# Attention and sparse feed-forward on one core: three banks for shifted scores, streamed row maxima, projections spread over the units

## What is computed

```python
q = (x @ wq).reshape(bsz, toks, NH, HD)      # NH 32, HD 16
k = (x @ wk).reshape(bsz, toks, NKV, HD)     # NKV 8
v = (x @ wv).reshape(bsz, toks, NKV, HD)
scores = jnp.einsum('bqgrd,bkgd->bgrqk', qg, k) / jnp.sqrt(...)
attn = jax.nn.softmax(scores, axis=-1)
out = jnp.einsum('bgrqk,bkgd->bqgrd', attn, v)
x = _layernorm(x + out.reshape(bsz, toks, NH * HD) @ wo)
idx = jnp.argmax(blk, axis=-1) + jnp.arange(0, INTER, SPARSITY)
x = _layernorm(x + einsum(relu(einsum(w1[idx], x)), w2t[idx]))
```

## Time and profile before

| | us |
|---|---|
| three timed runs | 1003.74, 1004.98, 1006.87 (median 1004.98) |
| the profiled execution | 998.58 |
| its span, first to last instruction | 996.8 |
| TensorE busy | 908.2 (91%) |
| VectorE busy | 562.4 (56%) |
| ScalarE busy | 442.9 (44%) |
| GpSimd busy | 193.1 (19%) |
| mean granted TensorE clock | 0.944 of 2.4 GHz |

### The profile page before, as it was taken

One profiled execution on the slowest core, in us unless ns is written; L12 is line 12 of the kernel. 1 busy time (PEld: TensorE's weight loads), 2 busy tenths in 40 slices (PEclk: granted clock), 3 DMA queues, 4 the chain that ended last, 5 costly groups with the idle time before them and its releaser, 6 DMA issues. The chain is left out here.

```text
span 996.8 us, 12134 instructions
## 1 busy us (share of the span) xinstructions
PE 908.2 (91%) x4472; PEld 533.0 (53%) x4472; DVE 562.4 (56%) x743; ACT 442.9 (44%) x821; POOL 193.1 (19%) x183
## 2 busy tenths in 40 slices
PE   5868999999899998999989975999999999999995
PEld 3745543333334333343333434777777777777774
DVE  4636567888656885468866533545563365326413
ACT  3302466777654775456765542322222222222231
POOL 6302003730210002100021002333321222122221
PEclk8889999999989998599988978999999999999998
DMA  8466535643342243323433124214030002001101
GB/s 249 160 205 240 169 110 159 175 123 91 91 117 69 76 134 80 97 85 79 135 82 109 34 97 102 82 44 155 14 116 11 1 3 103 2 1 43 42 1 42
DMA packets 50858, 92.99 MB, mean 93 GB/s; under 512 B 5648, under 2 KB 13840, under 8 KB 50288
## 3 DMA queue, kind: packets, MB, share of 16 engines
q1 hardware_dynamic: 49312, 87.05, 29.3%
q0 software_dynamic: 1488, 5.16, 1.9%
HBM read 56.80 MB, written 34.87 MB: 92 GB/s over the span
## 5 line engine op out<-in xcount | busy, mean ns | idle before, releaser
L509 DVE TENSOR_REDUCE neg_max<-ps_max 128x2 f32<-128x1024 f32 x256 | 302.9, 1217 | 90.1 <-PE ps_max L670 89.7
L486 ACT ACTIVATE probs<-ps_st 128x512 f32<-128x512 f32 x496 | 270.2, 595 | 142.6 <-PE ps_st L707 139.7
L707 PE MATMUL ps_st<-q,k 50*128 50x512 f32 x496 | 181.9, 511 | 28.5 <-ACT probs L486 27.6
L707 PEld LDWEIGHTS ps_st<-q,k 50*128 50x128 f32 x496 | 71.9, 192 | 203.1 <-ACT probs L486 156.8
L670 PE MATMUL ps_max<-k,q 48*128 48x512 f32 x512 | 152.8, 452 | 14.0 <-DVE neg_max L509 9.2
L721 PE MATMUL ps_pv<-probs,v 128*32 128x512 f32 x1024 | 147.3, 649 | 5.9 <-ACT probs L486 2.3
L978 POOL TENSOR_TENSOR g_l<-picked,g_h 128x512 fp32r<-128x512 f32 x56 | 73.1, 1306 | 286.9 <-ACT g_h L1017 286.9
L1003 ACT ACTIVATE mask_t<-ps_t 128x512 bf16<-128x512 bf16 x56 | 33.4, 597 | 163.6 <-PE ps_t L1199 163.6
L1211 PE MATMUL ps_h<-xt_h,w_h 128*128 128x512 f32 x224 | 93.8, 419 | 8.0 <-ACT relu L1010 8.0
L1073 DVE TENSOR_REDUCE top<-ps_prep 128x14 f32<-128x448 f32 x62 | 38.6, 623 | 99.0 <-PE ps_prep L1188 98.8
L670 PEld LDWEIGHTS ps_max<-k,q 48*128 48x128 f32 x512 | 75.6, 199 | 28.9 <-DVE neg_max L509 13.5
(11 more groups left out here) (159 smaller groups left out, 1141.2 us busy)
## 6 DMA issues: line engine op xcount, KB each, us to landing
q_stacks<-parts SPq DMA_DIRECT2D x48, 256.0 KB
q<-q_stacks SPq DMA_DIRECT2D x64, 192.0 KB, 3.6
sums<-stage SPq DMA_DIRECT2D x32, 256.0 KB, 3.4
k<-k_stacks SPq DMA_DIRECT2D x64, 96.0 KB, 3.1
x_raw<-xT SPq DMA_DIRECT2D x16, 256.0 KB, 8.5
yf<-after_attention SPq DMA_DIRECT2D x4, 1024.0 KB, 5.3
w_raw<-w POOLq DMA_DIRECT2D x16, 224.0 KB, 3.1
w_raw<-w SPq DMA_DIRECT2D x14, 256.0 KB, 2.9
```

The lines of the kernel that those rows point to most:

```text
L486: nc.scalar.activation(probs[kt % 2][:, r], score_bank(n, r), ACT.Exp, scale=float(HD) ** -0.5).then_inc(exp_done, 1)
L509: nc.vector.tensor_reduce(neg_max[n % 2][:, i // 2, :, i % 2], ps_max[i % 2][:], AX.X, ALU.max, negate=True).then_inc(max_red, 1)
L707: nc.tensor.matmul(score_bank(n, r), k_[n % QR][64 * a:64 * a + ROWS, kt * P:(kt + 1) * P], q[n % QR][64 * a:64 * a + ROWS, j, :], start=T ...
```

## The change

`_attend` is written anew in most of its orders; what is computed stays. PSUM in the loop is now `ps_pair` (two banks), `ps_one`, `ps_st` with three banks, `ps_pv`, `ps_x`. Tile i of the shifted scores may start when the exponential of tile i - 3 is done. The row-maximum tiles are one stream over all units: tiles 3m and 3m + 1 go to `ps_pair` and are reduced together, tile 3m + 2 to `ps_one`, alone; one such matmul stands behind each shifted one, 33 tiles ahead of the step's own. The tasks are ordered k, q, v, and only items 0 and 1 are projected ahead of the loop. The other 12 tasks and the 12 output tiles are groups, one per unit (`GROUPS`), each cut in pieces of four matmuls at the end of steps 2, 3 and the next unit's step 0. Output tiles stand in units 14 to 17, 19 to 22 and 28 to 31. The low parts of x for items 1 to 3 and the high parts for items 2 and 3 are made on GpSimd. Scaling and splitting w1 take another order on GpSimd: item 0's scaling, all of w1, item 1's, item 2's. `load_unit` waits for the last shifted score of the buffer's old unit instead of its last weighing. Part of SBUF is laid over other memory.

```diff
-        ps_max = [ps(f"ps_max{j}", [P, 2, S]) for j in range(2)]
-        ps_st = [ps(f"ps_st{j}", [P, S]) for j in range(2)]
-        ps_pv = ps("ps_pv", [P, S])
-        ps_x = ps("ps_x", [P, S])
-        bank = [(*ps_st, ps_pv)[i % 3] if i < FRONT else ps_x for i in range(LAST)]
+        ps_pair, ps_one = ps("ps_pair", [P, 2, S]), ps("ps_one", [P, S])
+        ps_st = [ps(f"ps_st{j}", [P, S]) for j in range(3)]
...
-        NEXT_X = {(0, 2): 1, (0, TASKS - 1): 2, (2, 3): 3}
-
-        LATE_AT = ((0, -1), (0, 2), (1, 0), (1, 2), (2, 0), (2, 2))
-
-        WO_AT = ((5, 0), (5, 2), (6, 0), (6, 2))
-        HIGH_AT = ((3, 2), (3, 3), (4, 0), (4, 1))
+
+        TURN_V = {6: 2, 13: 3}
+        GROUPS = {}
+        for o in range(TASKS):
+            GROUPS[o] = ("task", 2, o)
+            GROUPS[7 + o] = ("task", 3, o)
+        for t in range(TT):
+            GROUPS[14 + t] = ("wo", 0, t)
+            GROUPS[19 + t] = ("wo", 1, t)
+            GROUPS[28 + t] = ("wo", 2, t)
+        SUMS_FROM = (0, 12, 20)
+        HIGH_AT = {(11, r): (0, r) for r in range(REP)} | {(18, 1): (1, 0), (18, 2): (1, 1), (18, 3): (1, 2),
+                                                          (19, 0): (1, 3)} | {(27, r): (2, r) for r in range(REP)}
...
+            for o in range(VTASK):
+                store_part(0, o)
+            load_unit(0)
             for k in range(KT):
                 load_x(2, k)
-            for b in range(NB - 1):
-                for s in range(TASKS):
-                    store_projection(b, s)
-                    if b == NB - 2 and s == SHIFT_TASK:
-                        send_shift(0)
-                    if b == 1 and s in (1, 3):
-                        load_unit(1 + (1, 3).index(s))
-                if b == 0:
-                    load_unit(0)
-                if b == 1:
-                    load_v(0)
-                    load_v(1)
-                    for k in range(KT):
-                        load_x(3, k)
+            load_unit(1)
+            store_v(0)
+            load_unit(2)
+            load_v(0)
+            load_v(1)
+            for o in range(VTASK):
+                store_part(1, o)
+            send_shift(0)
+            store_v(1)
...
+            def row_max(tile):
+
+                dve.wait_ge(max_mm, tile + (2 if tile % 3 == 0 else 1))
+                old = (tile + 1) // TILES - 3
+                if old >= 0:
+                    dve.wait_ge(max_split, old + 1)
+                at = tile % RING
+                if tile % 3 == 0:
+                    nc.vector.tensor_reduce(neg_max[:, at:at + 2], ps_pair[:], AX.X, ALU.max,
+                                            negate=True).then_inc(max_red, 1)
+                else:
+                    nc.vector.tensor_reduce(neg_max[:, at:at + 1], ps_one[:], AX.X, ALU.max,
+                                            negate=True).then_inc(max_red, 1)
+
+            def row_maxima(begin, end):
+
+                for tile in range(begin, end):
+                    if tile % 3 == 1:
+                        row_max(tile - 1)
+                    elif tile % 3 == 2:
+                        row_max(tile)
...
-            def scores(n, i, a):
-
-                if n >= NU:
+            def scores(tile):
+
+                if tile >= NT:
                     return
-                if a == 0:
-                    if i == 0:
-                        pe.wait_ge(unit_in[n % QR], LOADS * DMA * (n // QR + 1))
-                    if 8 * n + i >= 2:
-                        pe.wait_ge(max_red, 8 * n + i - 1)
-                t, j = i // 2, i % 2
-                mm = nc.tensor.matmul(ps_max[i % 2][:, a], q[n % QR][64 * a:64 * a + STACK, j, t * P:(t + 1) * P],
-                                      k_[n % QR][64 * a:64 * a + STACK, :], start=True, stop=True)
-                if a == 1:
-                    mm.then_inc(max_mm, 1)
+                n, i = divmod(tile, TILES)
+                t, j, a = i // 4, i // 2 % 2, i % 2
+                if i == 0:
+                    pe.wait_ge(unit_in[n % QR], LOADS * DMA * (n // QR + 1))
+                if tile >= 3:
+                    pe.wait_ge(max_red, 2 * (tile // 3) - (tile % 3 < 2))
+                dst = ps_one[:] if tile % 3 == 2 else ps_pair[:, tile % 3]
+                nc.tensor.matmul(dst, q[n % QR][64 * a:64 * a + STACK, j, t * P:(t + 1) * P],
+                                 k_[n % QR][64 * a:64 * a + STACK, :], start=True, stop=True).then_inc(max_mm, 1)
...
-                if i < 2:
-                    pe.wait_ge(evacuated, FRONT - 2 + i)
-                elif n < NU - 2 or (n, kt) == (NU - 2, 0):
-                    pe.wait_ge(exp_done, i - 1)
-                    if r == 2 and n == NU - 2:
-                        pe.wait_ge(max_red, 8 * NU)
+                if i < 3:
+                    task_taken(pe, EARLY - 4 + i)
                 else:
-                    pe.wait_ge(exp_done, i - 3)
+                    pe.wait_ge(exp_done, i - 2)
...
+                    step = n * TT + kt
+                    ahead = 4 * step + 33
                     scores_t(n, kt, 0)
-                    if n == 0 and kt == 0:
-                        scores(2, 0, 0)
-                    scores(n + 2, 2 * kt, 1)
+                    scores(ahead)
                     scores_t(n, kt, 1)
-                    if kt or n:
-                        weigh(*divmod(n * TT + kt - 1, TT))
-                    if not b and (g, kt - 1) == LATE_AT[0]:
-                        turn_v(NB - 1)
-                    if not b and (g, kt) in LATE_AT:
-                        pe.wait_ge(shift_ready, n + 1 + (kt > 1))
-                        project(NB - 1, LATE_AT.index((g, kt)))
-                    if b and (g, kt) in WO_AT and n < NU - 2:
-                        project_out(b - 1, WO_AT.index((g, kt)), n + 1 + (kt > 1))
+                    scores(ahead + 1)
                     scores_t(n, kt, 2)
-                    scores(n + 2, 2 * kt + 1, 0)
+                    scores(ahead + 2)
+                    if step:
+                        weigh(*divmod(step - 1, TT))
                     scores_t(n, kt, 3)
-                    scores(n + 2, 2 * kt + 1, 1)
-                    scores(*divmod(8 * (n + 2) + 2 * kt + 2, 8), 0)
-                    if n == NU - 2 and (g, kt) in WO_AT:
-                        project_out(b - 1, WO_AT.index((g, kt)), n + 1 + (kt > 1))
+                    scores(ahead + 3)
+                    if kt == 0:
+                        group(n - 1, 8, 12)
+                    if kt == 1 and n + 1 < NU:
+                        if n == 0:
+                            pe.wait_ge(v_ready, 2)
+                        else:
+                            pe.wait_ge(shift_ready, n + 1)
+                            turned_free(pe, n - 1)
+                        turn_max(n + 1)
+                    if kt == 2:
+                        group(n, 0, 4 if n + 1 < NU else 6)
+                    if kt == 2 and n in TURN_V:
+                        pe.wait_ge(shift_ready, n + 2)
+                        turn_v(TURN_V[n])
+                    if kt == 3:
+                        group(n, 4 if n + 1 < NU else 6, 8 if n + 1 < NU else 12)
...
+            def group(n, begin, end):
+
+                kind, b, i = GROUPS.get(n, ("none", 0, 0))
+                if kind != "none" and begin == 0 and n + 1 < NU:
+                    pe.wait_ge(shift_ready, n + 2)
+                if kind != "none" and begin == 0 and n + 1 == NU:
+                    turned_free(pe, n - 1)
+                if kind == "task":
+                    project(b, i, begin, end)
+                if kind == "wo":
+                    project_out(b, i, begin, end)
...
+            add_tile(NB - 2, TT - 1)
+            variance(NB - 2)
+            norm(NB - 2)
```

597 lines of the change are left out of this document (328 added, 269 removed).

## The result

The changed kernel takes **1066.5 us** (median of four runs, 1051.8 to 1073.8) against 1004.5 for the kernel before (1003.7 to 1006.9): 1.053 times the time before, interval 1.042 to 1.064. The forecast was 983.7 us, faster, in a range of 952 to 1012. The sign was wrong, and the time lies 54 us above the range. The ratio is of fast runs alone: two of the four, the profiled one among them, are slower than the others at a lower mean clock (0.900 and 0.904 against 0.913 and 0.924). The profiled execution took 1073.8 us, span 1072.0. Against the span of before, 996.8, that is +75.2, the upper end of what the change costs, and it divides into stages.

The account below looks back on a forecast made before the run. Two score banks were taken to bound a plain unit (3.10 us chain per step), VectorE second. Start -29, loop +1.7 and end +6 gave 977.3 us, and 6.4 from profiled run to median made 983.7, range 952 to 1012.

Parts of the forecast that it names:

- Part 4: Half-clock stalls in the loop: 31.4 us are such events; with `att` cast later, no such wait is left.
- hand-followed chain: Twelve row-maximum tiles followed over three steps in the loop, weighings included: 9.33 us together, 3.11 per step.
- Part 1: Loop, three score banks and three row-maximum tiles: step 3.11 us (was 3.13), plain unit 13.05 (12.52 before).
- four rounds: Loop's rounds of a pair (A, B) and single C: 1.77 us without weighing; with it 2.03, 2.36, 3.17 (between A, B).
- Part 2: Loop's 24 groups of 12 matmuls in three pieces: 2.8 us per projection group, 3.3 per output tile.
- Part 3: Start, six projections leaving the front: unit 0 lands at 43 us, first exponential at 75 (68 to 90), -29.
- Part 5: End, between loop and feed-forward: the last output tile's work and the store of x1 follow the loop, +6 us.
- (c): Rival: the half clock stays by a new wait, +20 us, 1004 us, no change; chance 0.12.
- (b): Rival, loop's hand-over: a pair's second tile starts a slot late, 0.24 us per round, 1022 us in all; chance 0.13.
- the rule that the prediction set beside this rival: TensorE: only weight loads are pulled ahead of matmuls in flight; by this rule (b) is the case.
- (a): Rival, loop: VectorE at its own pace, weighings hidden behind full banks; plain unit 11 us, 922 us in all; chance 0.12.
- (d): Rival, start: the front gains only half, first exponential at 90 us, 998.7 us in all, still faster; chance 0.10.

Follow-up runs that it names:

- e1: The changed kernel with the next unit's shift sent ahead of the reciprocals on SyncE's queue, as in the kernel before; 1036.9 us, 1.031 times before.
- w1: The changed kernel with the weighing never between the two tiles of a pair, the shift left behind the reciprocals; 1021.2 us, 1.012 times before.
- e2: e1 with the weighing of every third step one tile forward, so that it never splits a pair; 996.2 us, 0.987 times before.
- e4: e1 with all twelve matmuls of a group in one piece at the end of step 2; 1041.3 us, 1.039 times before.
- e5: e2 with VectorE's part of a group earlier: output tile's addition ahead of step 1's maxima, projection's part between their halves; 1030.5 us, 1.025 times before.
- h1: g1 with ScalarE's casts of the second batch item's `att` one step later each; 981.7 us, 0.976 times before.
- b1: The kernel before with only the swap that puts the reciprocals' broadcast ahead of the shift on SyncE's queue; 1038.2 us, 1.028 times before.
- e6: e5 with item 3's loads of x behind unit 3's shift, and GpSimd's loads behind its casts for item 2; 1017.1 us, 1.001 times before.
- g3: g1 with row maxima over 256 of each tile's 512 columns, so the output differs; 961.6 us in one run.
- g1: e2 with e6's two moves of loads and without e5's moves on VectorE; 989.8 us, 0.983 times before.
- h2: h1 with VectorE's normalisation of two batch items cut into four tiles, one per step; 975.2 us, 0.968 times before.

## Why the prediction was wrong

Loop lengths of the profiled executions, the time at half clock in them, and how many waits they hold:

| | span | loop | at half clock | waits of TensorE of 0.7 to 1.3 us | over 1.3 us |
|---|---|---|---|---|---|
| before | 996.8 | 485.7 | 64.0 | 2 | 4 |
| after | 1072.0 | 572.9 | 153.9 | 39 | 5 |
| e1 | 1038.7 | 537.2 | 96.0 | 43 | 3 |
| w1 | 1023.3 | 523.4 | 109.9 | 14 | 5 |
| e2 | 992.1 | 490.6 | 52.8 | 18 | 3 |
| e4 | 1038.8 | 540.6 | 76.1 | 33 | 4 |
| e5 | 1027.6 | 528.4 | 136.9 | 14 | 8 |
| h1 | 980.2 | 483.2 | 52.9 | 15 | 2 |
| b1 | 1036.0 | 520.4 | 133.1 | 2 | 4 |

- **Part 4 is the step that failed.** It said that "no such wait is left in my reading" and took 31.4 us of stalls and half clock out of the loop. Instead 28.2 us of waits for the shift came in, and 153.9 us at half clock, at 0.40 another 62. Without these two the loop is 572.9 - 28.2 - 62 = 483 us (491 at a price of 0.35), and the forecast, which had neither, was 487.7. So the rest of the sum of the loop holds to about 5 us, if only in total (the plain unit was put 0.4 us too short), and the miss there is this part: 31.4 assumed gone, 90 found. It failed in two ways.
- *The queue.* The order on SyncE's queue was read for where the shift stands, not for what stands in front of it. For the reciprocals the prediction asked only when `att` is cast. The kernel before has the two calls in the other order, and e1, e2 against w1, and b1 show that the swap alone is worth 22 to 30 us in either kernel. The Trainium skill (DMA: Bandwidth & Descriptors, Queues, rings and completion order) says that each DMA engine takes one queue's descriptors in order and that a transfer's signal lands after every earlier write of that engine. By this rule a shift behind a megabyte lands with the megabyte, and the traces above agree, 12 to 13 us in the changed kernel and 11.3 in b1.
- *The clock.* The earlier trace rows showed one low stretch behind a wait of 3.20 us, and I took long waits for the only cause. The hand-followed chain itself said that TensorE would wait about once in three steps for a pair. I gave that its length in us and nothing more. In e1, with only two waits over 3 us left in the loop, 96 us of it are at half clock, and in e2, which takes out 25 of the waits of 0.7 to 1.3 us and none of the long ones, 52.8. All four runs of each bear it out: by their mean clocks the half clock in the whole span is 142 to 164 us in e1 and 88 to 146 in e2. The Trainium skill (TensorE: Matmul & The Clock Gate, A second HAM failure mode: psum-queue depth-cycling) describes short idle times between groups of matmuls, while banks are cycled, as enough to bring the clock down; e1 against e2 agrees. It is not their number alone: e5 has 14 such waits and 136.9 us at half clock, e4 has 33 and 76.1, and the kernel before has 77 waits of 0.15 to 0.4 us in its loop and keeps the clock beside them.
- **Part 1, the plain unit.** Forecast 13.05, wrong if over 13.7; measured 13.46 (580.30 to 593.76) in unit 27, the only plain one at full clock. Units 24 to 26, which the prediction named, took 18.5, 21.4 and 15.9 us at mean clocks of 0.58, 0.75 and 0.80, and the second holds the wait of 7.41 us; by the prediction's own sign they are wrong. In e1 the same units take 16.9, 13.6 and 13.6, the last two at full clock. The four rounds as VectorE shows them in unit 27 and 28:

```profile
584.43 1.23 DVE L602 TENSOR_REDUCE neg_max<-ps_pair 128x2 f32<-128x1024 f32 x1 [1.63 <-PE ps_pair L765]
...
586.52 1.23 DVE L602 TENSOR_REDUCE neg_max<-ps_pair 128x2 f32<-128x1024 f32 x1 [0.27 <-PE ps_pair L765]
...
588.61 1.22 DVE L602 TENSOR_REDUCE neg_max<-ps_pair 128x2 f32<-128x1024 f32 x1
...
590.92 1.22 DVE L602 TENSOR_REDUCE neg_max<-ps_pair 128x2 f32<-128x1024 f32 x1 [0.49 <-PE ps_pair L765]
...
594.19 1.23 DVE L602 TENSOR_REDUCE neg_max<-ps_pair 128x2 f32<-128x1024 f32 x1 [1.15 <-PE ps_pair L765]
```

  They are 2.09, 2.09, 2.31 and 3.27 us, where the prediction had 1.77, 2.03, 2.36 and 3.17. Three of four hold to 0.1; the round without a weighing was put 0.3 too short, and at 1.33 such rounds in a unit that alone is 0.4, the amount by which the unit is longer. The 0.3 lies between the start of the pair's matmuls (585.71, below) and their reduction (586.52): 0.81 us, where 0.48 was counted. The estimate for the 512-wide maximum (0.69) holds: 683 ns.

```profile
585.71 0.51 PE L765 MATMUL ps_pair<-k,q 48*128 48x512 f32 x2
```

- **Part 2, the groups.** A unit with a projection takes 15.6 to 15.7 us at full clock, forecast 13.05 + 2.8 = 15.85; one with an output tile 15.9 or 17.1, forecast 16.35. Right. What was missing is the normalisation in one block, 2.55 us of waiting in the changed kernel and the clock behind it.
- **Part 3, the start.** Forecast -29, measured -18.2. The first store was issued at 13.1 (forecast 12.5), but unit 0's load only at 42.9, when the five parts had landed (39), and unit 0 was there for TensorE at 48.55 (17.29 us of waiting) and not at 43. The shift of unit 0 was issued at 77.4 and not at 71, and the first exponential came at 85.9. The stores of item 0 share the transfers with more loads than the sum had: e6, which moves GpSimd's loads out of their way, has unit 0 at 40.70 and its first exponential at 79.3. The upper bound of 90 for "the front gains half" held it.
- **Part 5, the end.** Forecast +6, measured +6.0: the first feed-forward matmul comes 9.2 us behind the last `stage` copy, with a wait of 9.28.
- **The rivals.** (c), the half clock stays by a new wait, was the right one in kind. It had 0.12 and +20 us, since it counted one or two events of the size seen before; the measured excess is 90. (b) was to decide from 13.8 us per unit on, and 13.46 is below; but what it feared is there in part. In the trace A and B of the round without a weighing start together at 585.71, so no slot is lost in their start, and the rule that the prediction set beside this rival does not hold here: a shifted score stands between A and B in the program, and it starts at 586.05. Yet their reduction comes 0.3 us later than counted, which lengthens this one round of the four. (a) found no support: even g3's plain units are 11.6 and 11.9 us. (d) came in part: the front gained 18.2 of 29 us. The range was built from the bounds of the unit and of the front, and none for a step that had been taken to be free of stalls; that is why the time lies outside it.

What stays open: which waits bring the clock down. Two pairs of kernels show that it stays up longer when the waits between A and B go (e1 and e2, the changed kernel and w1); no run isolates their length or spacing. e2, g1, h1 and h2 keep 53 to 64 us of half clock in the loop, in other places in each, and single runs of one kernel lie up to 28 us apart (e6).

## What to carry to other kernels

On each queue that the change touches, list what stands directly ahead of the transfer on which the bound engine waits: here a short transfer behind a megabyte came 11 to 12 us after its issue, together with it. If the bound engine's clock depends on its activity, a chain that gives it a wait of 0.9 us in every third step can cost more than the waits' sum, as here: price the same unit at either clock from the trace, and put that into the range. And where two tiles are reduced together, let nothing long stand between the matmuls that fill them.
